# Routing weights of an expert layer: from a spreading matmul to a store and broadcast loads

## The chip, the cores and the metric

The kernel runs on one core of a Trainium2 chip. The metric is the device time of one execution in microseconds (us), as the median of several executions. Everything is float32 in memory; "F32R" tiles are float32 values rounded to what TensorE multiplies in one pass, so that a product of two such tiles split in a high and a low part takes three matmuls.

## The reference

Three layers work on 32 sequences of 128 tokens of width 128 (4096 tokens). The first is a state-space mixer, the second a cross attention with 16 heads, the third a layer of experts; each ends in a residual sum and a layer norm. The change lies in the third:

```
scores = sigmoid(xf @ gate_w.T)                  # 16 experts
# two of four groups of experts stay open, the best 4 experts of those are taken
topk_w = topk_w / (topk_w.sum(-1) + 1e-20) * 2.5
cw     = (one_hot(topk_idx) * topk_w).sum(1)     # 16 weights per token, 12 of them zero
act    = silu(xf @ Wg) * (xf @ Wu)               # 16 experts of 64 units
y      = einsum(act, cw, Wd) + shared expert     # 128 units, no weight
out    = layernorm(x + (x + y))
```

All experts are computed for all tokens; the routing weight `cw` scales the 64 units of each expert before the product with `Wd`.

## The kernel before, in words

The 32 sequences are worked in 8 groups of 4 (512 tokens); in the expert stage a tile is 128 units by 512 tokens. The units are cut into 9 chunks (`NC`) of 128: chunk 0 is the shared expert, chunks 1 to 8 hold two experts each. Five engines run their own in-order programs, tied by semaphores only.

For each chunk c, **TensorE** (`up`, from L1952) makes the gate product and the up product, three matmuls each (L1957), into two PSUM banks each (`GG`, `UU`), and for c > 0 one matmul more (L1962) that spreads the two rows of routing weights over 64 rows each into a third pair of banks (`WW`). The left operand of that one is a constant 0/1 matrix `spread`, the right one `cwT`, the transposed routing weights. Two chunks later `down` (L1965) multiplies the finished hidden chunk with the down weights (L1973). So TensorE's order is up(c), down(c-2). **ScalarE** makes silu of the gate bank (L1879). **VectorE** (`hidden`) multiplies silu with the up bank (L1912), waits for that result, and multiplies it with the spread weights (L1916).

The routing of group g+1 is made between the chunks of group g. `x2T` transposes the next tokens (L1781) after chunk 2, from a tile `xs` that SyncE loaded from the SBUF tensor `x2` (L1845); ScalarE copies and rounds the transposed tokens (L1679, L1682), VectorE makes their low part (L1699); `expert_logits` (L1788) follows chunk 3. On VectorE `expert_scores` and `rank_groups` stand behind chunk 3, `select_experts` (L1747 to L1757) behind chunk 5, `share_weights` (L1767 to L1776) behind chunk 7. Its last two instructions split `cw` in two parts. TensorE transposes both parts (`transpose_weights`, L1796) after up(g+1, 0); ScalarE copies the result to `cwT` (L1694). After the 9 chunks VectorE makes residual sum and statistics (L124, L131, L135), GpSimd normalises (L141 to L148), SyncE stores (L1851).

In the expert stage SyncE's program of group g is: load `xs` of group g+2, wait for the normalised group g, store it. The loop over groups is `pairs`: three turns of a hardware loop of two groups, and two groups unrolled.

The routing of group 0 is made in the last group of the attention stage: VectorE routes ahead of `invert`, TensorE transposes at the end of `group`, ScalarE copies after `context`. In the attention stage GpSimd also prepares for the experts: `prepare_pool` in group 4 builds `spread` in the memory of the raw weights, `load_weights` in group 5 starts the loads of the expert weights, `split_weights` splits the up and gate weights into high and low parts (L1669, L1672).

`Sem.at(g, k)` is the count that a semaphore has once step k of group g is done.

Of the kernel before, what the change touches and what calls it, by code (L numbers as in the profile page):

```python
# [44 lines left out]
SPREAD, PREPARED = 6, 12  # L45
# [940 lines left out]
def attention(nc, t, d, psum, a, e):  # L986
# [12 lines left out]
    with ExitStack() as ctx:  # L999
# [97 lines left out]
        def _(pool):  # L1097
# [80 lines left out]
        def _(act):  # L1178
            for s in (a_exp, a_mt, a_ctx, *d_m, *d_ms, e.a_x, e.a_l, e.a_c, e.a_f):
                s.prime(act)  # L1180
# [32 lines left out]
            def group(g, par, left):  # L1213
# [32 lines left out]
                if not left:  # L1246
                    copy_weights(act, e, 0, 0)
# [143 lines left out]
        def _(pe):  # L1391
            for s in (p_v, p_s, p_t, p_u, p_c, p_mt, p_o, p_b, e.p_x, e.p_l, e.p_c, e.p_u, e.p_w):
                s.prime(pe)
# [124 lines left out]
            def group(g, par, left):  # L1518
# [23 lines left out]
                weigh(g, par, 2, 1)  # L1542
                if left >= 2:
                    values(g + 2, par)
# [10 lines left out]
                if not left:  # L1555
                    transpose_weights(pe, e, 0)
# [36 lines left out]
def expert_tensors(ctx, nc, t, psum, a):  # L1593
# [9 lines left out]
    e.w_raw = sb("w_raw", [P, 2, NC, P])  # L1603
    e.w_up = sb("w_up", [P, 2, 2, NC, P], F32R)
# [4 lines left out]
    e.spread = sb("spread", [P, CHUNKS, P], F32R)  # L1609
    e.before = sb("before", [P, 4, 4])  # L1610
    e.xT_hl = [sb("xT_hl_c0", [P, 2, GT], F32R)]
    e.cwT = [sb(f"cwT{k}", [P, GT], F32R) for k in range(2)]
# [10 lines left out]
    e.cw, e.cw_hl = sb("cw", [P, GS, EXPERTS]), sb("cw_hl", [P, GS, 2, EXPERTS], F32R)  # L1623
# [3 lines left out]
    e.p_u, e.p_w = sem("up_mm", NC), sem("weight_mm", CHUNKS)  # L1627
    e.a_x, e.a_l, e.a_c, e.a_f = sem("x2T_hi"), sem("logit_tanh"), sem("cwT_ready"), sem("x2T_f32")
    e.v_x, e.v_sc, e.v_grp, e.v_sel = sem("x2T_lo"), sem("scores_ready", 2), sem("groups_ranked", 13), sem("select_dve", 18)
# [3 lines left out]
def prepare_pool(pool, e, pick):  # L1633

    before, steps = e.before, e.steps
    pool.memset(pick[:, :, :, :], 1.0).then_inc(steps, 1)
    pool.memset(before[:, :, :], 1.0).then_inc(steps, 1)
    pool.wait_ge(steps, 2)

    pool.affine_select(out=pick[:, :, :, :], in_=pick[:, :, :, :], compare_op=ALU.is_equal, fill=0.0, base=0,  # L1640
                       pattern=[[-2, CHUNKS], [-1, 2], [0, EI]], channel_multiplier=1).then_inc(steps, 1)
    pool.affine_select(out=before[:, :, :], in_=before[:, :, :], compare_op=ALU.is_gt, fill=0.0, base=0,
                       pattern=[[1, 4], [-1, 4]], channel_multiplier=0).then_inc(steps, 1)
    pool.wait_ge(steps, 4)
    pool.affine_select(out=pick[:, :, :, :], in_=pick[:, :, :, :], compare_op=ALU.not_equal, fill=1.0, base=-EXPERTS,
                       pattern=[[-2, CHUNKS], [-1, 2], [0, EI]], channel_multiplier=1).then_inc(steps, 1)
    pool.wait_ge(steps, 5)
    pool.tensor_copy(e.spread[:, :, :], pick[:, :, :, :].rearrange("p c e i -> p c (e i)")).then_inc(steps, 1)
    for cwT in e.cwT:
        pool.memset(cwT[:, :].bitcast(F32), 0.0).then_inc(steps, 1)  # L1650
# [13 lines left out]
def split_weights(pool, e):  # L1664
# [5 lines left out]
    pool.wait_ge(steps, 10)  # L1670
# [90 lines left out]
def share_weights(dve, e, g):  # L1761

    def step(k, ins):
# [8 lines left out]
    step(15, dve.scalar_tensor_tensor(e.cw[:, :, :], e.chosen[:, :, :], SCALE, bc(e.wsum[:, :, None], [P, GS, EXPERTS]),  # L1772
                                      ALU.mult, ALU.mult))
# [18 lines left out]
def transpose_weights(pe, e, g):  # L1792
    pe.wait_ge(e.v_sel.sem, e.v_sel.at(g, 17))
# [270 lines left out]
```

## Time and profile before

| what | us |
|---|---|
| median of 3 executions | 636.02 (634.12 to 638.72) |
| the profiled execution | 634.59 |
| its span, first to last instruction | 632.9 |
| TensorE busy in the span | 576.1 (91%) |
| VectorE busy | 481.5 (76%) |
| ScalarE busy | 279.6 (44%) |
| GpSimd busy | 205.7 (33%) |
| mean granted TensorE clock | 0.969 of full |

Busy shares are means over the three stages. The expert stage runs from 430.65 us, its first gate matmul, to the end. The page's row of memory traffic shows 114 to 205 GB/s in the attention stage and mostly 0 to 34 GB/s in the expert stage.

### The profile page before, as it was taken

What the parts mean: (1) busy time and instruction counts of PE and PEld (TensorE: products, weight loads), DVE (VectorE), ACT (ScalarE), POOL (GpSimd) and SP (SyncE); (2) the same over time, 40 slices, a digit from 0 to 9 for tenths busy, and PEclk for the clock granted to TensorE, in tenths of its full rate; (3) what the DMA queues carried; (4) which work ended last, traced back from release to release, by engine and by line L of the source; (5) the groups of instructions that cost most, each with busy time, mean ns of one, the idle gap of its engine ahead of it and who ended that gap; (6) DMA issues with size and microseconds to landing.
All of it is one profiled execution on the core that took longest, in us unless ns stands there. A gap on an engine that the chain in (4) does not pass through costs nothing. (4 is left out here: it accounts for less than half of the span.)

```text
span 632.9 us, 17897 instructions
## 1 busy us (share of the span) xinstructions
PE 576.1 (91%) x6280; PEld 480.9 (76%) x6280; DVE 481.5 (76%) x1174; ACT 279.6 (44%) x548; POOL 205.7 (33%) x256
## 2 busy tenths in 40 slices
PE   5769999999999866999999999788999999999994
PEld 5647876887888655787878877567888888888884
DVE  2858888888988758687787788665787787887863
ACT  2356645645655423565575555343233223233220
POOL 4233224314412574325434547732022022021022
PEclk9969999999999967999999999799999999999998
DMA  7122122022111473544545545000010010110000
GB/s 225 58 66 86 48 67 66 33 66 66 53 58 40 114 205 89 142 136 143 156 144 151 140 124 171 5 4 34 2 34 6 28 33 0 33 33 0 18 18 17
DMA packets 43086, 46.13 MB, mean 73 GB/s; under 512 B 5056, under 2 KB 31328, under 8 KB 43024
## 3 DMA queue, kind: packets, MB, share of 16 engines
q1 hardware_dynamic: 41104, 42.57, 22.5%
q0 software_dynamic: 704, 1.92, 1.0%
q10 hardware_dynamic: 1216, 0.79, 0.5%
q8 instruction: 41, 0.67, 0.4%
q14 instruction: 21, 0.17, 0.1%
HBM read 32.48 MB, written 10.94 MB: 69 GB/s over the span
## 5 line engine op out<-in xcount | busy, mean ns | idle before, releaser
L1957 PE MATMUL bank<-xT_hl_c,w_up 128*128 128x512 f32 x432 | 118.1, 409 | 2.4 <-ACTq L67 2.4
L141 POOL TENSOR_TENSOR rstd<-mv,norm_c 128x4 f32<-128x4 f32 x24 | 5.2, 216 | 289.2 <-DVE mv L135 188.4
L1879 ACT ACTIVATE sg<-bank 128x512 f32<-128x512 f32 x72 | 42.9, 596 | 105.0 <-PE bank L1957 105.0
L1957 PEld LDWEIGHTS bank<-xT_hl_c,w_up 128*128 128x128 f32 x432 | 76.1, 189 | 15.8 <-ACTq L67 2.6
L1282 DVE TENSOR_REDUCE nmax<-bank 128x4 f32<-128x512 f32 x112 | 72.0, 685 | 20.6 <-PE bank L1439 19.3
L1186 ACT ACTIVATE prob<-bank 128x512 f32<-128x512 f32 x128 | 69.4, 595 | 40.8 <-PE bank L1439 33.0
L1973 PEld LDWEIGHTS bank<-w_down,hid 128*128 128x128 f32 x576 | 74.4, 191 | 5.9 <-issue 0.5
L1973 PE MATMUL bank<-w_down,hid 128*128 128x128 f32 x576 | 75.6, 275 | 0.0
L1912 DVE TENSOR_TENSOR gu<-sg,bank 128x512 f32<-128x512 f32 x64 | 43.9, 685 | 21.4 <-PE bank L1957 10.2
L1429 PE MATMUL bank<-neg_i,mask 64*128 64x256 bf16 x512 | 51.2, 279 | 9.1 <-DVE nmax L1290 3.0
L1916 DVE TENSOR_TENSOR hid<-gu,bank 128x512 f32<-128x512 f32 x64 | 44.0, 688 | 6.5
L477 ACT ACTIVATE expo<-rows,neg_sums 128x128 f32<-128x128 f32 x128 | 40.8, 390 | 11.2 <-DVE mix L855 11.1
L422 PE MATMUL bank<-xhl,w_feat 128*128 128x512 f32 (+1 forms) x96 | 31.4, 452 | 9.0 <-DVE b_rot L814 5.1
L1479 PE MATMUL bank<-prob,ones_s 128*32 128x128 f32 x1024 | 34.6, 276 | 0.5 <-ACT prob L1186 0.5
L1429 PEld LDWEIGHTS bank<-neg_i,mask 64*128 64x128 bf16 x512 | 16.4, 95 | 23.8 <-issue 9.8
L1483 PE MATMUL bank<-prob,v_d 128*32 128x128 f32 x1024 | 34.4, 275 | 0.0
L919 PE MATMUL bank<-c_rot,b_rot 128*128 128x256 f32 x128 | 32.9, 378 | 0.0
L1479 PEld LDWEIGHTS bank<-prob,ones_s 128*32 128x32 f32 x1024 | 26.0, 109 | 5.7 <-issue 2.2
L916 PE MATMUL bank<-plain 96*128 96x512 f32 x96 | 30.0, 420 | 0.0
L908 PEld LDWEIGHTS bank<-w_x,xhl 128*128 128x128 f32 x192 | 26.8, 189 | 3.8 <-issue 1.2
L422 PEld LDWEIGHTS bank<-xhl,w_feat 128*128 128x128 f32 (+1 forms) x96 | 16.9, 186 | 16.7 <-DVE c_rot L818 7.6
L908 PE MATMUL bank<-w_x,xhl 128*128 128x256 f32 x192 | 28.6, 285 | 0.0
(220 smaller groups left out, 1184.7 us busy)
## 6 DMA issues: line engine op xcount, KB each, us to landing
rows<-sum_rows_scratch SPq DMA_DIRECT2D x32, 256.0 KB, 3.2
k_stack<-k_scratch SPq DMA_DIRECT2D x32, 128.0 KB, 2.8
q_stack<-q_scratch SPq DMA_DIRECT2D x32, 128.0 KB, 2.7
k_scratch<-k_part SPq DMA_DIRECT2D x16, 192.0 KB, 2.4
q_scratch<-q_part SPq DMA_DIRECT2D x16, 192.0 KB, 2.4
x<-xT_in SPq DMA_DIRECT2D x8, 256.0 KB, 8.6
mask<-mask_in SPq DMA_DIRECT2D x8, 256.0 KB, 3.0
xres<-x_in SPq DMA_DIRECT2D x8, 256.0 KB, 3.7
```

The source lines that it names most:

```text
L422: mm = pe.matmul(bank[0:m, :], w[:, i, :], xhl[:, par, v, :, 1:], start=(n == 0), stop=(n == 2))
L477: act.activation(expo[:, b % 2, h, :], rows[:, b, h, :], ACT.Exp, bias=upto_s[:, bass.ds(g * GS + b, 1), h]).then_inc(s_exp.sem, 1)
L908: mm = pe.matmul(bank[:, shift * D_INNER:(shift + 1) * D_INNER], xhl[:, par, a, b, 1 - shift:P + 1 - shift], w_x[:, v, :], start=(n == 0), ...
L1186: act.activation(prob[:, b % 2, ORDER[n], :, :], (TT0, TT1)[n % 2][:, :], ACT.Exp, scale=XD ** -0.5)\
L1282: dve.tensor_reduce(nmax[:, b, 4 * u:4 * u + 4], (SS0, SS1)[n % 2][:, :].rearrange("p (i k) -> p i k", i=4), AX_X, ALU.max, negate=True).t ...
L1429: pe.matmul(banks[j][:, :].rearrange("p (i h k) -> p i h k", i=4, h=2)[:, :, half, :], mask[rows, par, b, kind + ver, :], bc(neg_i[rows, N ...
L1479: mm = pe.matmul(U1[32 * u:32 * u + 32, 0:P], ones_s[:, 4 * b + i, :, :].rearrange("p r c -> p (r c)"), prob[:, b % 2, u, i, :], start=(b ...
L1879: act.activation(sg[:, k, :], GG[k][:, :], ACT.Silu).then_inc(a_s.sem, 1)
L1912: dve.tensor_tensor(dst, sg[:, k, :], UU[k][:, :], ALU.mult).then_inc(v_gu.sem, 1)
L1916: dve.tensor_tensor(hid[:, c, :], gu[:, k, :], WW[(c - 1) % 2][:, :], ALU.mult).then_inc(v_hid.sem, 1)
L1957: mm = pe.matmul(bank[:, :], w_up[:, which, a, c, :], xT_hl[par][:, v, :], start=(n == 0), stop=(n == 2))
L1973: mm = pe.matmul(PO[:, b * P:(b + 1) * P], hid[:, c, b * P:(b + 1) * P], w_down[:, c, :], start=(c == 0 and b == 0), stop=(c == NC - 1), s ...
```

## The change

- `spread`, its building on GpSimd, the spreading matmuls and the split of `cw` in two parts are gone; `cw` is transposed as it is, to 16 rows.
- ScalarE copies the 16 x 512 transposed weights to SBUF and stores them to DRAM from its own queue. SyncE loads them back as `share`: each row to 64 partitions, in eight loads of 256 KB per group (for each of four pairs of chunks one load to partitions 0 to 63, one to 64 to 127). The loads stand ahead of the load of `xs` in SyncE's program, and each pair of loads waits until VectorE has used the pair's old content.
- VectorE multiplies by `share` instead of by a PSUM bank.
- Gate and up products have three banks each.
- `select_experts` stands behind chunk 4 (before 5), `share_weights` behind chunk 5 (before 7), `transpose_weights` and the copy behind chunk 7 (before: after up(g+1, 0)). In the last attention group the transposes stand ahead of the last two products `weigh(g, par, 3, ...)`, the copy ahead of `context`.
- VectorE's loop over the groups is unrolled.

```
@@ attention, gpsimd / scalar / tensor, last groups @@
                 if left == 2:
-                    pool.wait_ge(e.steps, SPREAD)
                     load_weights(pool, d, e)
...
-                        prepare_pool(pool, e, e.w_raw[:, 0, 0:CHUNKS, :].rearrange("p c (x y) -> p c x y", x=2))
+                        prepare_pool(pool, e)
...
+                if not left:
+                    copy_weights(act, e, 0, 0)
                 context(g)
...
                 weigh(g, par, 2, 1)
+                if not left:
+                    transpose_weights(pe, e, 0)
                 if left >= 2:
                     values(g + 2, par)
                 weigh(g, par, 3, 1)
...
 def prepare_pool(pool, e):
-    (memset, two affine_select and a copy of 128x1024 for spread, two memsets of cwT)
     pool.memset(before[:, :, :], 1.0).then_inc(steps, 1)
...
 def copy_weights(act, e, g, par):
     act.wait_ge(e.p_c.sem, e.p_c.at(g))
-    act.wait_ge(e.p_w.sem, e.p_w.at(g - 2, CHUNKS - 1))
-    act.activation(e.cwT[par][0:32, :], e.PF[0:32, :], ACT.Copy).then_inc(e.a_c.sem, 1)
+    act.wait_ge(e.d_stored.sem, e.d_stored.at(g - 1))
+    act.activation(e.cw_rows[:, :], e.PF[0:EXPERTS, :], ACT.Copy).then_inc(e.a_c.sem, 1)
+    act.wait_ge(e.a_c.sem, e.a_c.at(g))
+    act.dma_start(e.cw_dram[par], e.cw_rows[:, :]).then_inc(e.d_stored.sem, 16)
...
 def share_weights(dve, e, g):
-    step(16, dve.tensor_copy(e.cw_hl[:, :, 0, :], e.cw[:, :, :]))
-    step(17, dve.tensor_tensor(e.cw_hl[:, :, 1, :], e.cw[:, :, :], e.cw_hl[:, :, 0, :].bitcast(F32), ALU.subtract))
...
-        GG, UU, WW, PF, PO = psum[0:2], psum[2:4], psum[4:6], psum[6], psum[7]
+        GG, UU, PF, PO = psum[0:3], psum[3:6], psum[6], psum[7]
@@ experts, sync @@
+            def load_shares(g, par):
+                sp.wait_ge(e.d_stored.sem, e.d_stored.at(g))
+                by_half = e.cw_dram[par].rearrange("(c j) t -> j c t", j=2)
+                for q, loaded in enumerate(d_share):
+                    sp.wait_ge(v_hid.sem, v_hid.at(g - 1, 2 * q + 1))
+                    for j in range(2):
+                        sp.dma_start(share[EI * j:EI * j + EI, 2 * q:2 * q + 2, :],
+                                     by_half[j, 2 * q:2 * q + 2].partition_broadcast(EI)).then_inc(loaded.sem, 16)
             def group(g, par, left):
+                if left:
+                    load_shares(g + 1, 1 - par)
                 if left == 2:
                     load(g + 2, par)
                 sp.wait_ge(g_out.sem, g_out.at(g, 3))
...
+            load_shares(0, 0)
             load(1, 1)
@@ experts, vector @@
-                    dve.wait_ge(p_w.sem, p_w.at(g, c - 1))
-                    dve.tensor_tensor(hid[:, c, :], gu[:, k, :], WW[(c - 1) % 2][:, :], ALU.mult)
+                    dve.wait_ge(d_share[(c - 1) // 2].sem, d_share[(c - 1) // 2].at(g))
+                    dve.tensor_tensor(hid[:, c, :], gu[:, k, :], share[:, c - 1, :], ALU.mult)
...
-            pairs(dve, group)
+            for g in range(NG):
+                group(g, g % 2, min(2, NG - 1 - g))
@@ experts, tensor @@
-                    pe.wait_ge(freed.sem, freed.at(g, c - 2))
+                    pe.wait_ge(freed.sem, freed.at(g, c - 3))
...
-                    pe.matmul(WW[(c - 1) % 2][:, :], spread[:, c - 1, :], cwT[par][:, :], start=True, stop=True)
...
+                    if left and c == 7:
+                        transpose_weights(pe, e, g + 1)
                 if left:
                     up(*nxt, 0)
-                    transpose_weights(pe, e, g + 1)
                 down(g, NC - 2)
```

## Rows read from the trace of the kernel before

**Rows 1.** Busy time per stretch: busy us (instructions) of PE, PEld, DVE, ACT, POOL; clock, DMA share, GB/s.
```profile
456.00:481.00 25.00, 25.00 (x155) 21.83 (x154) 20.62 (x66) 7.32 (x13) 3.25 (x4) 1.00 0.07 23
```

**Rows 2.** Chain that ended last, 552 to 602 us: start us, us, what.
```profile
552.29 0.61 PE bank L1796 x4
...
597.10 1.40 PE bank L1957 x6
598.49 0.23 PE bank L1962
...
601.02 0.44 PE bank L1796 x4
```

**Rows 3.** Timeline of VectorE in the second group: start us, us, engine, line, [idle before].
```profile
459.16 0.68 DVE L124 SCALAR_TENSOR_TENSOR res<-x,bank 128x512 f32<-128x512 f32 x1
...
462.96 0.69 DVE L1699 TENSOR_TENSOR xT_hl_c<-rest,xT_hl_c 128x512 fp32r<-128x512 f32 x1 [0.19 <-ACT xT_hl_c L1682]
...
469.00 0.69 DVE L1912 TENSOR_TENSOR gu<-sg,bank 128x512 f32<-128x512 f32 x1 [0.29 <-PE bank L1957]
...
471.82 0.22 DVE L1747 TENSOR_TENSOR open_<-biased,penalty 128x64 f32<-128x64 f32 x1
...
473.93 0.69 DVE L1912 TENSOR_TENSOR gu<-sg,bank 128x512 f32<-128x512 f32 x1 [0.30 <-ACT sg L1879]
...
476.76 0.19 DVE L1767 TENSOR_SCALAR chosen<-marked 128x64 f32<-128x64 f32 x1
...
477.91 0.22 DVE L1772 SCALAR_TENSOR_TENSOR cw<-chosen,wsum 128x64 f32<-128x64 f32 x1
...
478.40 0.23 DVE L1776 TENSOR_TENSOR cw_hl<-cw,cw_hl 128x64 fp32r<-128x64 f32 x1
```

**Rows 4.** Timeline of TensorE and of ScalarE in the second group, same columns.
```profile
460.96 0.60 PE L1781 MATMUL bank<-ident,xs_c 128*128 128x128 f32 x4
...
479.58 0.59 ACT L1694 ACTIVATE cwT<-bank 32x512 fp32r<-32x512 f32 x1 [0.54 <-PE bank L1796]
```

**Rows 5.** Timeline of SyncE's queue: issues in the first stage, and at the expert stage's start.
```profile
25.73 0.56 SPq L456 DMA_DIRECT2D sum_rows_scratch<-sum_rows  x1
27.60 1.76 SPq L461 DMA_DIRECT2D rows<-sum_rows_scratch  x4
...
430.62 4.05 SPq L1845 DMA_DIRECT2D xs_c<-x  x2
```

**Rows 6.** The broadcast loads of the first stage (one tile's view), and a stretch of them.
```profile
DMA to landing us min/median/max: 3.0/3.2/5.6
...
30.00:31.00 1.00, 1.00 (x5) 0.69 (x4) 0.51 (x2) 0.98 (x2) 0.32 (x1) 1.00 0.98 363
```

**Rows 7.** A stretch of loads that land on 32 or on 16 partitions each.
```profile
238.00:240.00 2.00, 0.78 (x18) 0.42 (x12) 2.00 (x4) 0.63 (x1) 1.19 (x1) 1.00 1.03 211
```

**Rows 8.** Issues by line: KB each, median us to landing.
```profile
xs_c<-x SPq DMA_DIRECT2D x7, 256.0 KB, 2.3
```

**Rows 9.** Timeline of GpSimd, VectorE and TensorE in attention groups 4 and 5.
```profile
375.98 0.95 POOL L1636 MEMSET w_raw<- 128x1024 f32 x1
...
381.73 0.20 POOL L141 TENSOR_TENSOR rstd<-mv,norm_c 128x4 f32<-128x4 f32 x1
...
398.38 5.23 POOL L1672 TENSOR_TENSOR w_up<-w_raw,w_up 128x1152 fp32r<-128x1152 f32 x2
...
401.12 2.54 DVE L1306 TENSOR_TENSOR npart<-nrest,npart 128x32 bf16<-128x32 f32 x1
...
403.81 0.38 PE L1503 MATMUL bank<-ident,npart 128*48 128x128 bf16 x2 [3.85 <-DVE npart L1306]
```

**Rows 10.** A stretch right after that wait of TensorE, columns as in Rows 1.
```profile
404.00:409.00 5.00, 5.00 (x38) 4.02 (x37) 1.21 (x2) 2.31 (x5) 4.25 (x4) 0.50 0.02 5
```

**Rows 11.** Timeline of TensorE and VectorE in the last attention group.
```profile
422.48 1.08 PE L1479 MATMUL bank<-prob,ones_s 128*32 128x128 f32 x32 [0.16 <-ACT prob L1186]
...
423.00 0.23 DVE L1772 SCALAR_TENSOR_TENSOR cw<-chosen,wsum 128x64 f32<-128x64 f32 x1
```

More of the change, by code:

```diff
@@ L44 @@
 SENTINEL, TAKEN = -3.0e38, 3.0e38
-SPREAD, PREPARED = 6, 12
+PREPARED = 6
 TWO_ONES = 1 + 0x3F80 / 2**23
@@ L1178, in _ @@
         def _(act):
-            for s in (a_exp, a_mt, a_ctx, *d_m, *d_ms, e.a_x, e.a_l, e.a_c, e.a_f):
+            for s in (a_exp, a_mt, a_ctx, *d_m, *d_ms, e.a_x, e.a_l, e.a_c, e.a_f, e.d_stored):
                 s.prime(act)
@@ L1391, in _ @@
         def _(pe):
-            for s in (p_v, p_s, p_t, p_u, p_c, p_mt, p_o, p_b, e.p_x, e.p_l, e.p_c, e.p_u, e.p_w):
+            for s in (p_v, p_s, p_t, p_u, p_c, p_mt, p_o, p_b, e.p_x, e.p_l, e.p_c, e.p_u):
                 s.prime(pe)
@@ L1554, in group @@
                 output(g)
-                if not left:
-                    transpose_weights(pe, e, 0)
             def first_scores(b, p):
@@ L1603, in expert_tensors @@
     e.w_raw = sb("w_raw", [P, 2, NC, P])
+    e.cw_rows = sb("cw_rows", [EXPERTS, GT])
+    e.cw_dram = nc.dram_tensor("cw_scratch", (2, EXPERTS, GT), F32, kind="Internal").ap()
     e.w_up = sb("w_up", [P, 2, 2, NC, P], F32R)
@@ L1608, in expert_tensors @@
     e.bias = sb("bias", [P, EXPERTS])
-    e.spread = sb("spread", [P, CHUNKS, P], F32R)
     e.before = sb("before", [P, 4, 4])
     e.xT_hl = [sb("xT_hl_c0", [P, 2, GT], F32R)]
-    e.cwT = [sb(f"cwT{k}", [P, GT], F32R) for k in range(2)]
     e.th16 = sb("th16", [P, GS, EXPERTS])
@@ L1669, in split_weights @@
         pool.tensor_copy(w_up[:, k, 0], w_raw[:, k]).then_inc(steps, 1)
-    pool.wait_ge(steps, 10)
+    pool.wait_ge(steps, 4)
     for k in range(2):
@@ L1815, in raw @@
             return ctx.enter_context(nc.semaphore(name))
-        w_up, w_down, spread, xT_hl, cwT = e.w_up, e.w_down, e.spread, e.xT_hl, e.cwT
+        w_up, w_down, xT_hl = e.w_up, e.w_down, e.xT_hl
         xT_hl.append(sb("xT_hl_c1", [P, 2, GT], F32R))
@@ L1822, in experts @@
         hid = sb("hid", [P, NC, GT])
+        share = sb("share", [P, CHUNKS, GT])
         res, stats, mv, rstd = t["res"], t["stats"], t["mv"], t["rstd"]
@@ L1827, in experts @@
         d_x, d_out = DmaSem(ctx, nc, "x2_staged"), DmaSem(ctx, nc, "out_stored")
-        p_x, p_u, p_w, a_c = e.p_x, e.p_u, e.p_w, e.a_c
+        d_share = [sem(f"share_loaded{q}", 1, 32) for q in range(CHUNKS // 2)]
+        p_x, p_u, a_c = e.p_x, e.p_u, e.a_c
         p_g, p_d, a_s = sem("gate_mm", NC), sem("down_mm", NC), sem("silu_ready", NC)
@@ L1841, in _ @@
             d_out.prime(sp)
+            for loaded in d_share:
+                loaded.prime(sp)
+            def load_shares(g, par):
[6 more added lines that the diff above has]
+                                     by_half[j, 2 * q:2 * q + 2].partition_broadcast(EI)).then_inc(loaded.sem, 16)
             def load(g, par):
@@ L1926, in group @@
                         rank_groups(dve, e, g + 1)
+                    if left and c == 4:
+                        select_experts(dve, e, g + 1)
                     if left and c == 5:
-                        select_experts(dve, e, g + 1)
-                    if left and c == 7:
                         share_weights(dve, e, g + 1)
@@ L1952, in up @@
             def up(g, par, c):
-                k = (par + c) % 2
-                for which, bank, freed, done in ((0, GG[k], a_s, p_g), (1, UU[k], v_gu, p_u)):
-                    pe.wait_ge(freed.sem, freed.at(g, c - 2))
+                for which, bank, freed, done in ((0, GG[c % 3], a_s, p_g), (1, UU[c % 3], v_gu, p_u)):
+                    pe.wait_ge(freed.sem, freed.at(g, c - 3))
                     for n, (a, v) in enumerate(((0, 0), (0, 1), (1, 0))):
@@ L1958, in up @@
                     mm.then_inc(done.sem, 1)
-                if c:
-                    pe.wait_ge(a_c.sem, a_c.at(g))
-                    pe.wait_ge(v_hid.sem, v_hid.at(g, c - 3))
-                    pe.matmul(WW[(c - 1) % 2][:, :], spread[:, c - 1, :], cwT[par][:, :], start=True, stop=True)\
-                        .then_inc(p_w.sem, 1)
             def down(g, c):
@@ L1985, in group @@
                         expert_logits(pe, e, g + 1)
+                    if left and c == 7:
+                        transpose_weights(pe, e, g + 1)
                 if left:
                     up(*nxt, 0)
-                    transpose_weights(pe, e, g + 1)
                 down(g, NC - 2)
```

39 lines of the change are left out of this document (13 added, 26 removed).

## The prediction

> **What bounds the kernel now.** I read the busy time per stretch first, then the chain of waits, then each engine's timeline in one group of the expert stage. TensorE is busy for 25.00 of 25.00 us in a stretch of that stage, VectorE for 20.62 [rows 1], so only what leaves TensorE's path or lands on it counts. The chain is TensorE alone: the transposes of the routing weights recur at 552.29 and, two groups later, at 601.02 [rows 2], a period of 24.37 us. A chunk on it is the gate and up products 1.40, the spreading matmul 0.23, and down; between 597.10 and 601.02 stand up, spread, down, up, so down is 3.92 - 1.40 - 0.23 - 1.40 = 0.89 [rows 2].
>
> **What is removed.** Eight spreading matmuls per group, 8 x 0.23 = 1.87 us, would leave a period of 22.5 if TensorE stayed the bound. VectorE loses two small instructions, 478.13 to 478.63 [rows 3], 0.5 us. Its multiplication doesn't get quicker: with one operand in PSUM it takes 0.69, with both in SBUF also 0.69 (L1699) [rows 3].
>
> **What is added, as a cycle.** I follow one group from the end of cw on VectorE (call it S, before at 477.91 + 0.22 = 478.13) to the S of the next group, because three new waits stand in that cycle one behind the other.
>
> 1. Transposes and ScalarE's copy: from the last routing instruction, 478.40 + 0.23, to the copy's end, 479.58 + 0.59, are 1.54 us [rows 3, 4].
> 2. Store and the issue of the first load: the first stage has the same pair, store issued at 25.73, first broadcast load at 27.60, 1.87 us [rows 5]. The load is issued at S + 3.4.
> 3. Eight loads of 256 KB, then, in the same queue, the 256 KB of xs that TensorE transposes for the next group but one. A broadcast load there lands 3.2 us after its issue in the median, and the stretch with several in flight moves 363 GB/s [rows 6], so 0.72 us of the 3.2 are data and 2.48 are fixed. With d us of data per load, xs lands at S + 3.4 + 2.48 + 9d = S + 5.9 + 9d. SyncE issues four loads in 1.76 us [rows 5], 0.44 each, so d decides as long as it is larger. The last pair also waits for VectorE's last chunk of the running group, three chunks behind S, some 4.2 us (3 x 1.41, below), which is over when its turn comes.
> 4. Transpose, two copies on ScalarE, start of L1699: 460.96 to 462.96, 2.00 us [rows 4, 3].
> 5. From there VectorE has one serial program to the next S. L1699, chunk 3 and the ranking: 462.96 to 469.00, 6.04. Chunk 4: half of 469.00 to 471.82, 1.41. Selection: 471.82 to 473.93, 2.11. Chunk 5: half of 473.93 to 476.76, 1.42. The shares: 476.76 to 478.13, 1.37. Sum 12.35 [rows 3].
>
> The new period is 5.9 + 9d + 2.00 + 12.35 = **20.24 + 9d**, if xs is what TensorE waits for. It is: behind the transposes TensorE has four ups and four downs before it needs xs, 0.44 + 4 x 1.40 + 4 x 0.89 = 9.6 us after S. Even at the highest rate of the trace, d = 0.72, xs lands at S + 12.4. Before, this load stood at the head of the group's program; now its issue comes some 7 us after S, and its data queue behind 2 MB.
>
> **The value of d.** No row has loads of 64 rows. Those of 128 rows moved 363 GB/s at a DMA share of 0.98 [rows 6]; those of 32 and of 16 rows (line 276) moved 211 GB/s at 1.03 [rows 7], the engines as full and the bytes fewer: 1.24 us per 256 KB. Between 0.72 and 1.24 I take 1.1, nearer to the narrow loads, because a load that reaches only half of the rows resembles them more, and the wider of them is half as wide. Period: 20.24 + 9.9 = 30.1, against 24.37.
>
> The Trainium skill has a rule on this, "SBUF — State Buffer", section "Door 1: The DMA port swizzle": 64 partitions reach 8 of the 16 ports, as 32 do, and two loads on the two halves run almost one after the other. Its table has 196 GB/s for 64 rows, d = 1.34, by which the same sum, clock term included, would give about 694 us.
>
> **The sum.** In group 0 the shares are loaded as the stage starts, ahead of xs of group 1. By the issue at 430.62 [rows 5], xs lands at 430.62 + 2.48 + 9.9 = 443.0, the first S is 2.00 + 12.35 later, 457.35, and the seventh six periods later, 457.35 + 6 x 30.14 = 638.2. What follows has no routing and TensorE sets it. Before, 31.9 us lay from the last transposes to the end (632.9 - 601.02); now the transposes stand one up, one down and one more up sooner (3.7) and eight spreading matmuls go (1.87): 33.7. The span ends at 671.9, +39.0.
>
> **The attention stage.** GpSimd's building of the spreading matrix stood ahead of its normalisation, 375.98 to 381.73 [rows 9]; nearly all of it goes, so that the weights load and split sooner. The second half of the split ran from 398.38 for 5.23 us while VectorE's small L1306 took 2.54, and TensorE waited 3.85 us for it [rows 9]. An earlier split holds VectorE for a shorter time; bounds 0 and 3.85, I take -2.5 (half of the 5.75 is swallowed by GpSimd's other waits). Against it, the transposes of group 0 now stand ahead of the last products, which began at 422.48, and wait for cw, finished at 423.23 [rows 11]; with 0.44 of their own they delay what follows by about 1.2. Net -1.3, bounds -3.85 and +1.2.
>
> **The clock.** TensorE would wait 15.8 - 9.6 = 6.2 us for xs in each group. After its wait of 3.85 us [rows 9] the granted clock of the next stretch is 0.50, the 1.2 GHz level [rows 10]. The work from xs to the scores then takes longer: an up and a down, 2.29, would cost 2.29 more. Bounds 0 and 2.3 per group; I take 1 in 7 groups, since VectorE's own work covers part: +7.
>
> **Costed at nothing.** The copy and the issue on ScalarE ahead of silu(8): ScalarE works 7.32 of 25 us [rows 1]; 0.6 per group if silu were late. VectorE's unrolled loop: it is hidden by the wait for xs; without that, not more than 0.3 per group, the gaps of its timeline [rows 3]. Three banks: TensorE can't run further ahead, since down(c-2) still waits for VectorE; no gain. The small weight store and the output store, behind xs in the queue, have a group's time.
>
> Profiled execution 634.59 + 39.0 - 1.3 + 7 = **679 us**; that execution lies 1.4 below the median shown, too little to correct for.
>
> **The rivals.**
> - *Full-rate loads* (0.15): the same late xs, but 64 rows run as 128 do, d = 0.72. Period 26.7, S at 453.9 and 614.3, end 648.0, and a wait of 2.8 us without a clock loss: 634.6 + 15.0 - 1.3 = 648. For it: 363 GB/s was reached with the same kind of source. Against it: rows 7.
> - *The halves never overlap* (0.13): a load to one half of the rows holds all engines until it is done, and 64 rows run at the 211 GB/s of the narrow loads, d = 1.24 [rows 7]. Period 31.4, S at 458.6 and 647.0, end 680.7; with the clock term 688. For it: the engines' full share in those rows. Against it: they contain loads of 16 rows. It is the rule of the Trainium skill's "SBUF — State Buffer", "Door 1: The DMA port swizzle", above.
> - *xs overtakes* (0.07): issued at S + 3.4 + 8 x 0.44 = S + 6.9 and landing 2.3 later [rows 8], it is there at 9.2, just in time. Then VectorE waits for the first pair of shares, S + 3.4 + 2.48 + 2d = 8.1, multiplies (0.6), makes residual and chunk 2 (459.16 to 462.96, 3.8) and the 12.35: period 24.9, no better than before, since routing behind chunks 3, 4 and 5 leaves TensorE little to do in the first half of a group. 634.6 + 6 x 0.5 - 1.9 - 1.3 = 634.
> - *Faster: TensorE stays the bound* (0.09): period 22.5, 8 x 1.87 = 15 us less, 634.6 - 15 - 1.3 = 618. It decides if xs is there by S + 9.6, that is d below 0.42 (620 GB/s in one queue), or if it overtakes and VectorE's serial part is 2.4 shorter than its rows make it. For it: VectorE has 4.4 us of idle time per 25 [rows 1], which three banks might let it use.
>
> **How the numbers follow.** The forecast has 0.56. Its own range, d from 0.9 to 1.2 with a clock term from 0 to 14, is 660 to 692. The range of 8 in 10 takes in both rivals on loads, from 644 (full rate and the whole gain of attention) to 695. Faster by over 1% 0.09, within 1% 0.07, slower 0.84; 1% is about what runs of this kernel, 634.12 to 638.72, tell from no change.
>
> **What would show it.** In the changed kernel: xs issued behind eight share loads and landing well over 2.3 us later; TensorE's transposes (L1781 before) waiting some 6 us per group for it, and VectorE's low part behind them; a period near 30; share loads at 210 to 260 GB/s with the DMA share near 1; a granted clock under 1 in the expert stage. A period under 25 with TensorE busy throughout would prove me wrong, and xs on time would prove the mechanism wrong.

## The result, and the profile after

The changed kernel takes 678.8 us in the median of 4 runs (675.77 to 679.85), against 635.53 for the kernel before on the same chip. The ratio is 1.0666, 95% interval 1.0632 to 1.0701: slower by 43 us. The forecast was 679. The profiled execution is one of 679.48 us with a span of 677.7.

Four views carry the reading. First busy time per stretch, columns as in [rows 1]: one whole period of the expert stage, the stretch in which its loads land, and the one after TensorE's wait.

```profile
456.07:487.41 31.34, 25.51 (x143) 21.68 (x143) 19.59 (x63) 7.38 (x13) 3.56 (x4) 0.89 0.37 86
...
462.70:471.30 8.60, 3.38 (x22) 2.60 (x20) 4.75 (x13) 0.60 (x1) 3.56 (x4) 0.91 0.98 213
...
472.00:477.00 5.00, 5.00 (x22) 4.42 (x20) 2.07 (x3) 1.78 (x3) 0.00 (x0) 0.55 0.18 52
```

TensorE, without a gap in [rows 1], now has work for 25.51 us of 31.34. While the loads land the DMA engines are full (0.98) and move 213 GB/s, close to the 211 GB/s of the narrow loads in [rows 7] and far from the 363 GB/s of [rows 6]. Behind the wait the granted clock is 0.55, near the lower of the two levels (1.2 GHz); in [rows 1] it was 1.00.

Second the waits: engine, line, what it waited for, us in total, times, longest. Third the issues by line, as in [rows 8], and the share of each line in the chain that ended last.

```profile
DVE xT_hl_c L1689 <- ACT xT_hl_c L1670: 39.7, 7, 7.0
PE bank L1769 <- DMA xs_c<-x: 34.5, 7, 5.3
...
DVE hid L1920 <- DMA share<-cw_scratch: 6.5, 7, 1.5
```

```profile
share<-cw_scratch SPq DMA_DIRECT2D x64, 256.0 KB, 5.6
...
xs_c<-x SPq DMA_DIRECT2D x7, 256.0 KB, 7.0
...
cw_scratch<-cw_rows ACTq DMA_DIRECT2D x8, 32.0 KB, 1.6
```

```profile
DMA xs_c<-x 7%; SPq L1840 5%; PE bank L1961 5%; PE bank L1972 3%; DVE gu L1916 2%; DVE hid L1920 2%; DMA cw_scratch<-cw_rows 1%; PE bank L1769 1%; PE bank L1776 1%; DVE marked L1747 1%; DMA share<-cw_scratch 1%; PE bank L1784 1%; ACT cw_rows L1682 1%; DVE top L1742 0%; DVE chosen L1758 0%
```

The waits that cost are not those for the new loads (6.5 us in seven groups) but those for xs, which queues behind them: 34.5 us on TensorE, 39.7 on VectorE one step later. The load that landed 2.3 us after its issue [rows 8] now takes 7.0, and it has the largest share of the chain.

Fourth the timelines of one cycle, VectorE, TensorE, ScalarE and SyncE, in the order of the forecast's steps; they answer to [rows 3 to 5].

```profile
455.79 0.22 DVE L1763 SCALAR_TENSOR_TENSOR cw<-chosen,wsum 128x64 f32<-128x64 f32 x1
...
456.07 0.60 PE L1784 MATMUL bank<-ident,cw 128*16 128x128 f32 x4
...
456.80 0.59 ACT L1682 ACTIVATE cw_rows<-bank 16x512 f32<-16x512 f32 x1 [2.11 <-PE bank L1784]
...
457.41 0.31 ACTq L1684 DMA_DIRECT2D cw_scratch<-cw_rows  x1
...
459.07 5.27 SPq L1840 DMA_DIRECT2D share<-cw_scratch  x8
...
464.61 0.54 SPq L1845 DMA_DIRECT2D xs_c<-x  x1
...
465.93 1.13 PE L1972 MATMUL bank<-w_down,hid 128*128 128x128 f32 x8 [0.98 <-DVE res L124]
...
471.68 1.11 PE L1769 MATMUL bank<-ident,xs_c 128*128 128x128 f32 x4 [4.62 <-DMA xs_c<-x]
472.44 2.91 PE L1961 MATMUL bank<-xT_hl_c,w_up 128*128 128x512 f32 x6
...
474.18 0.69 DVE L1689 TENSOR_TENSOR xT_hl_c<-rest,xT_hl_c 128x512 fp32r<-128x512 f32 x1 [5.15 <-ACT xT_hl_c L1670]
487.41 0.60 PE L1784 MATMUL bank<-ident,cw 128*16 128x128 f32 x4
```

S is 455.79 + 0.22 = 456.01. xs is issued 8.6 us later and TensorE can start on it at 471.68, S + 15.7. From transposes to transposes it is 31.34 us; from the first cw of the stage at 455.79 to the seventh at 641.60 the mean period is 30.97.

The attention stage, same view of GpSimd, VectorE and TensorE, answers to [rows 9, 11].

```profile
375.16 0.11 POOL L1635 MEMSET before<- 128x16 f32 x1
...
393.94 5.22 POOL L1660 TENSOR_TENSOR w_up<-w_raw,w_up 128x1152 fp32r<-128x1152 f32 x2
...
399.67 0.19 DVE L1305 TENSOR_TENSOR npart<-nrest,npart 128x32 bf16<-128x32 f32 x1
...
400.62 0.29 PE L1502 MATMUL bank<-ident,npart 128*48 128x128 bf16 x2
...
418.46 0.60 PE L1784 MATMUL bank<-ident,cw 128*16 128x128 f32 x4 [0.96 <-DVE cw L1763]
...
427.04 6.76 PE L1961 MATMUL bank<-xT_hl_c,w_up 128*128 128x512 f32 x18 [2.79 <-ACTq L67]
```

L1305, which took 2.54 us in [rows 9], takes 0.19, and TensorE's 3.85 us of waiting are gone. A wait of 0.96 us for `cw`, by the sooner transposes, is new.

### The profile page after: what moved, and what is told of

Its sections match the earlier page's. It is cut to its first block and busy times, and to the rows that moved or that the text cites. A ratio compares the mean times of both kernels' runs of the same rounds, so it can differ in the third digit from the quotient of the medians.

```text
span 677.7 us, 17557 instructions
## 1 busy us (share of the span) xinstructions
PE 579.4 (85%) x6216; PEld 478.5 (71%) x6216; DVE 477.2 (70%) x1158; ACT 279.6 (41%) x548; POOL 202.6 (30%) x250
## 5 line engine op out<-in xcount | busy, mean ns | idle before, releaser
L1961 PE MATMUL bank<-xT_hl_c,w_up 128*128 128x512 f32 x432 | 128.9, 438 | 2.8 <-ACTq L67 2.8
L1961 PEld LDWEIGHTS bank<-xT_hl_c,w_up 128*128 128x128 f32 x432 | 83.5, 207 | 18.3 <-ACTq L67 2.9
L1972 PEld LDWEIGHTS bank<-w_down,hid 128*128 128x128 f32 x576 | 77.2, 198 | 18.1 <-issue 6.3
L1185 ACT ACTIVATE prob<-bank 128x512 f32<-128x512 f32 x128 | 69.4, 594 | 41.5 <-PE bank L1438 32.4
L1972 PE MATMUL bank<-w_down,hid 128*128 128x128 f32 x576 | 79.1, 282 | 6.5 <-DVE res L124 5.8
L1920 DVE TENSOR_TENSOR hid<-gu,share 128x512 f32<-128x512 f32 x64 | 47.4, 741 | 8.4 <-DMA share<-cw_scratch 6.5
L477 ACT ACTIVATE expo<-rows,neg_sums 128x128 f32<-128x128 f32 x128 | 40.8, 390 | 11.1 <-DVE mix L855 11.0
L1769 PE MATMUL bank<-ident,xs_c 128*128 128x128 f32 x28 | 7.8, 433 | 34.5 <-DMA xs_c<-x 34.5
L1689 DVE TENSOR_TENSOR xT_hl_c<-rest,xT_hl_c 128x512 fp32r<-128x512 f32 x8 | 5.5, 688 | 39.7 <-ACT xT_hl_c L1670 39.7
L1769 PEld LDWEIGHTS bank<-ident,xs_c 128*128 128x128 f32 x28 | 5.0, 217 | 35.8 <-DMA xs_c<-x 20.4
```

The costliest lines, as they stand in the source:

```text
L477: act.activation(expo[:, b % 2, h, :], rows[:, b, h, :], ACT.Exp, bias=upto_s[:, bass.ds(g * GS + b, 1), h]).then_inc(s_exp.sem, 1)
L1185: act.activation(prob[:, b % 2, ORDER[n], :, :], (TT0, TT1)[n % 2][:, :], ACT.Exp, scale=XD ** -0.5)\
L1920: dve.tensor_tensor(hid[:, c, :], gu[:, k, :], share[:, c - 1, :], ALU.mult).then_inc(v_hid.sem, 1)
L1961: mm = pe.matmul(bank[:, :], w_up[:, which, a, c, :], xT_hl[par][:, v, :], start=(n == 0), stop=(n == 2))
L1972: mm = pe.matmul(PO[:, b * P:(b + 1) * P], hid[:, c, b * P:(b + 1) * P], w_down[:, c, :], start=(c == 0 and b == 0), stop=(c == NC - 1), s ...
```

## The experiments

Ratios are to the kernel before, run on the same chip.

**The order of the queue.** The load of xs is issued ahead of the eight share loads, in the loop and at the start.

```
-                if left:
-                    load_shares(g + 1, 1 - par)
                 if left == 2:
                     load(g + 2, par)
+                if left:
+                    load_shares(g + 1, 1 - par)
...
+            load(1, 1)
             load_shares(0, 0)
-            load(1, 1)
```

> The changed kernel with one edit: SyncE issues the load of xs ahead of the eight share loads, in the loop and at the stage's start. Theory (xs is late because it queues behind 2 MB of share loads): TensorE's wait for xs, 4.6 to 5.1 us a group, goes, the granted clock of the expert stage comes back to 1.0, and the next limit is the first pair of shares and VectorE's serial part, a period of 24 to 25 us against 31.3; total 626 to 634, below the changed kernel by some 48. Rival A (the order of the routing, behind chunks 3, 4 and 5, costs the time, and the wait for xs only hides it): the period falls to 28 at best, total 650 or more. Rival B (the share loads' own traffic slows everything): hardly any change, 670 to 679.

It took 633.67 us, ratio 0.9975 (0.9950 to 1.0000), not clearly different from the kernel before. One place in a program is the whole loss of 43 us. TensorE has no wait for xs left, its load lands 2.4 us after the issue, and the mean period is 24.63. The place decides two things at once, which this run doesn't separate: what xs queues behind, and when it is issued, which is no longer after the wait for the store. The share loads were as slow as in the changed kernel: a landing every 1.17 us in both. VectorE's waits for them are what is left, and in one period the clock is back at 1.00:

```profile
xs_c<-x SPq DMA_DIRECT2D x7, 256.0 KB, 2.4
...
DVE hid L1920 <- DMA share<-cw_scratch: 6.4, 8, 1.5
...
474.10:499.30 25.20, 23.20 (x142) 19.67 (x142) 20.13 (x63) 7.32 (x13) 3.57 (x4) 1.00 0.43 106
```

**Width of a load, first try.** Each load fills one chunk, two rows of weights to all 128 partitions, the source given as 2 x 64 x 512; alone, and with xs first.

```
-                    for j in range(2):
-                        sp.dma_start(share[EI * j:EI * j + EI, 2 * q:2 * q + 2, :],
-                                     by_half[j, 2 * q:2 * q + 2].partition_broadcast(EI)).then_inc(loaded.sem, 16)
+                    for c in (2 * q, 2 * q + 1):
+                        two = e.cw_dram[par, 2 * c:2 * c + 2, :]
+                        sp.dma_start(share[:, c, :], two[:, None, :].to_broadcast([2, EI, GT])).then_inc(loaded.sem, 16)
```

> The changed kernel with one edit: the same eight loads of 256 KB and the same contents, but each load brings one chunk to all 128 partitions instead of two chunks to 64. Theory (d, the data time of a load, is set by how many partitions it reaches): a load takes 0.72 to 0.8 us instead of the 1.16 between two landings of the changed kernel, xs lands 3.2 to 4 us sooner, the period is 20.24 + 9 x 0.75 = 27 us, total 640 to 652. Rival (reading the same 2 KB of DRAM 64 times sets the rate, or the issue on SyncE of 0.65 us): loads stay at 1.1 us or more, total 672 to 680.

> Both edits: xs first and share loads to 128 partitions. Theory: with xs out of the way the rate of the share loads matters only for VectorE's wait for the first pair of shares, about 1 us a group: 1 to 3 us less than xs first alone, 624 to 631. Rival (the loads' rate matters for itself): 8 us or more below xs first alone.

They took 936.55 us, ratio 1.4722 (1.4654 to 1.4790), and 795.71, ratio 1.2527 (1.2465 to 1.2589). Every range was missed, by some 165 us at the least. The busy time per stretch, and the tile's view of the issues (engine, count, duration in ns min/median/max), of the first of the two:

```profile
427.00:500.00 73.00, 31.39 (x160) 26.11 (x159) 18.87 (x55) 9.86 (x17) 2.69 (x3) 0.71 0.10 38
```

```profile
L1840 SPq DMA_DIRECT2D share<-cw_scratch x64: 498/4979/7296, 426.9 to 901.9; - x64
```

The engines are 0.10 busy on the mean of 16 and move 38 GB/s while everything waits, and one issue takes up to 7.3 us. The Trainium skill, "DMA: Bandwidth & Descriptors", "Why a DMA increments its semaphore by 16 and not by 1", says that a transfer is split over the largest number of engines, up to 16, that divides the slowest dimension of source and destination both. By that the source's slowest dimension of 2 leaves 2 engines of 16, 0.125, and 0.10 agrees; which engines were busy no row here shows. By the rate alone these two runs changed another thing than the width, and they say nothing of it.

**Width of a load, second try.** One row of weights goes to all 128 partitions, so that both sides have 128 as their slowest dimension. The second expert of each pair is left out, so the output is not that of the reference.

```
+                    for c in (2 * q, 2 * q + 1):
+                        sp.dma_start(share[:, c, :], e.cw_dram[par, 2 * c, :].partition_broadcast(P)).then_inc(loaded.sem, 16)
```

> The changed kernel, with its 256 KB loads one row to all 128 partitions instead of two rows to 64 (the weights of each pair's second expert are left out and the first's used in their place). Theory (the half-width destination is what makes a load take 1.16 us on the queue): spacing falls to about 0.72 us, as in the full-width load that moved 363 GB/s [rows 6]; the staging load lands 8 x 0.44 = 3.5 us sooner, its wait on TensorE falls from 4.6 to about 1.1 us, period 31.3 - 3.5 = 27.8, time 679 - 7 x 3.5 = 654 (648 to 660). Rival A (256 KB written take 1.16 us whatever the width): 679 (675 to 683). Rival B (a broadcast source keeps it off most of the engines, as in the run with two rows in one load): above 750.

It took 662.94 us, ratio 1.0438 (1.0390 to 1.0487), between the theory and rival A. The stretch from the first landing to the last:

```profile
459.70:466.30 6.60, 3.76 (x24) 2.98 (x22) 4.75 (x13) 1.00 (x2) 2.52 (x3) 0.96 0.98 280
```

With the engines as full as before (0.98) they move 280 GB/s instead of 213; over all groups a load lands every 0.89 us instead of 1.17. The mean period is 28.52, 2.45 shorter: 7 x 0.28 = 1.96 for the spacing, the rest for a first landing 3.0 to 3.4 us after its issue instead of 3.6 to 4.0. So the width costs, as the theory had it, though a load now also reads one row of weights instead of two, which no run separates. The gain was seven tenths of the 3.5 forecast. The 363 GB/s [rows 6] are the mean of 1 us; the three loads that land around it come 0.77 and 0.80 us apart, so 0.72 was too low a price even there.

**Another queue for xs.** ScalarE issues the load behind the second silu of the next group.

```
                     silu(*nxt, 1)
+                if left == 2:
+                    act.wait_ge(p_x.sem, p_x.at(g))
+                    act.dma_start(xs[:, par, :, :], x2[:, bass.ds((g + 2) * GS, GS), :]).then_inc(d_x.sem[par], 16)
```

> The changed kernel, with the staging load issued by ScalarE behind the second silu of the next group, at nearly the same time (S + 8.9) but in another queue. Theory (the load waits for its turn behind the eight share loads in SyncE's queue): in a queue of its own it shares the engines and lands about S + 12 to 13 instead of S + 15.6, TensorE's wait falls by about 3 us of 4.6, time 679 - 7 x 3 = 658 (650 to 665). Rival A (it is the engines that are busy, in the order in which the requests came, whatever queue they came from): 679 (675 to 683). Rival B (ScalarE's issue holds up the silus): above 685.

It took 665.76 us, ratio 1.0463 (1.0417 to 1.0510), 0.8 above the theory's range. In the group that answers to the one above (S = 456.72):

```profile
459.78 5.34 SPq L1840 DMA_DIRECT2D share<-cw_scratch  x8
...
462.92 0.60 ACTq L1897 DMA_DIRECT2D xs_c<-x  x1
...
469.75 1.11 PE L1769 MATMUL bank<-ident,xs_c 128*128 128x128 f32 x4 [2.51 <-DMA xs_c<-x]
```

TensorE's wait for xs falls from 4.62 to 2.51 us. Two things changed, not one: ScalarE issued xs at S + 6.2, where the expectation had S + 8.9 and the changed kernel S + 8.6, and from issue to landing it still takes 6.8 us, against 7.0. So the run doesn't tell the queue from the sooner issue in the 13 us gained. What the other queue does is seen in the order: xs lands 2.8 us ahead of the last share load (2.2 to 3.4 over the groups) instead of 0.3 behind it, and the share loads spread to one per 1.30 us. It shares the same busy engines (0.93 of them from 463.5 to 472.4 us). The Trainium skill, "DMA: Bandwidth & Descriptors", "Queues, rings and completion order", has each engine take packets from its queues in turn; this run agrees.

**Routing where it was.** Selection, shares, transposes and copy go back to their old places; loads and multiplication stay.

```
-                    if left and c == 4:
+                    if left and c == 5:
                         select_experts(dve, e, g + 1)
-                    if left and c == 5:
+                    if left and c == 7:
                         share_weights(dve, e, g + 1)
```

(and so for the transposes and the copy, behind the next group's first up and first silu).

> The changed kernel with the routing put back to its old places: selection behind chunk 5, shares behind chunk 7, transposes after the gate and up products of the next group's chunk 0, copy after its silu. Everything else stays. Theory (the cycle through store, share loads and xs is the bound): weights that are ready two chunks later start the loads later, VectorE then waits some 4 to 5 us for the first pair of shares, period 33 to 35, total 692 to 710. Rival (routing sooner is what costs): period falls, total below 670.

It took 703.1 us (two runs), ratio 1.1056 (1.0987 to 1.1124), as expected. The sooner routing is worth 24 us here:

```profile
PE bank L1769 <- DMA xs_c<-x: 32.2, 7, 5.9
DVE hid L1919 <- DMA share<-cw_scratch: 30.6, 7, 4.6
```

The wait for xs stays what it was, and VectorE waits for the first shares on top of it. The two waits stand in the same cycle one behind the other.

**The clock.** TensorE makes 18 spare matmuls into the free bank while it waits for xs.

```
+                pe.wait_ge(a_c.sem, a_c.at(g - 1))
+                for _ in range(18):
+                    pe.matmul(e.PF[:, :], w_up[:, 0, 0, 0, :], xT_hl[1 - par][:, 0, :], start=True, stop=True)
                 pe.wait_ge(d_x.sem[par], d_x.at(g, par))
-                pe.wait_ge(a_c.sem, a_c.at(g - 1))
```

> The changed kernel, with 18 spare matmuls of 128x512 on TensorE while it waits for the staging load. Theory (about 1.3 us of each period is the half clock after that wait: transposes 1.11 for 0.60, up 2.91 for 1.64): the granted clock stays at full speed, period 31.3 - 1.3 = 30.0, time 679 - 7 x 1.3 = 670 (667 to 674). Rival A (what is late lies on the transfers and VectorE, not on TensorE's speed): 679 (676 to 682). Rival B (18 x 0.22 = 4 us of matmuls outlast the wait of 4.6 us after some groups): 680 to 690.

It took 667.42 us, ratio 1.0517 (1.0468 to 1.0565). The last row is busy time per stretch, from the spare matmuls to the end of the period.

```profile
466.65 4.45 PE L1955 MATMUL bank<-xT_hl_c,w_up 128*128 128x512 f32 x18
471.63 0.66 PE L1769 MATMUL bank<-ident,xs_c 128*128 128x128 f32 x4 [0.53 <-DMA xs_c<-x]
472.05 1.66 PE L1963 MATMUL bank<-xT_hl_c,w_up 128*128 128x512 f32 x6
...
466.60:487.00 20.40, 19.66 (x114) 16.26 (x113) 13.94 (x51) 4.97 (x10) 3.57 (x4) 1.00 0.23 54
```

xs is no sooner than in the changed kernel, but the granted clock behind it is 1.00 and the up takes 1.66 us instead of 2.91. Spare work made the kernel 11 us faster by the medians; the mean period is 29.13, so the half clock had cost 1.84 per group. What lies between xs and the scores is TensorE's own work, at whatever clock it gets.

**The attention stage.** The removed preparation on GpSimd is put back, for nobody's use, with the waits that it had.

```
-PREPARED = 6
+SPREAD, PREPARED = 6, 12
...
+    pool.memset(pick[:, :, :, :], 1.0).then_inc(steps, 1)
...
+    pool.tensor_copy(e.spread[:, :, :], pick[:, :, :, :].rearrange("p c e i -> p c (e i)")).then_inc(steps, 1)
+    for cwT in e.cwT:
+        pool.memset(cwT[:, :].bitcast(F32), 0.0).then_inc(steps, 1)
```

> The changed kernel, with GpSimd's removed preparation put back (the spread matrix is built and two tensors are cleared, for nobody; loading and splitting the expert weights wait for it as before). Theory (this work is what delayed the split weights, VectorE and TensorE in the attention's last groups): stage start goes back from 427.0 to 430.6, time 679 + 3.6 = 682.5 (681.5 to 684). Rival (the sooner routing and the other order of the last group made the 3.6 us): 679 (678 to 680).

It took 682.83 us, ratio 1.0751 (1.0712 to 1.0790), above the changed kernel's interval; by the medians that is 4.0 us. The old wait is back:

```profile
375.59 0.95 POOL L1638 MEMSET w_raw<- 128x1024 f32 x1
...
403.63 0.38 PE L1503 MATMUL bank<-ident,npart 128*48 128x128 bf16 x2 [3.31 <-DVE npart L1306]
...
431.82 4.43 PE L1975 MATMUL bank<-xT_hl_c,w_up 128*128 128x512 f32 x18 [2.79 <-ACTq L67]
```

From the start of GpSimd's preparation to the start of the expert stage the three kernels have 54.67 (before), 51.88 (after) and 56.23 us (this one). By these three traces the removed work is worth 4.35, and the new order of the last group costs 56.23 - 54.67 = 1.56. The 1.56 is loose: in the eleven other kernels with the attention stage of the changed one the stretch is 51.5 to 52.8 us in ten and 54.45 in one.

**No loads at all.** In the changed order the share loads are made for the first group alone; the others multiply by its weights.

```
+                    if first:
                         for j in range(2):
...
+                    else:
+                        sp.sem_inc(loaded.sem, 32)
```

> The changed kernel in the order that it has, but the share loads are made for the first group alone (the later groups multiply by the first group's weights); their places in SyncE's queue, the waits for the store and for the buffers stay. Theory (everything that the change lost, it lost to these transfers): the staging load lands 2.4 us after its issue, no wait for it on TensorE, period about 24.5, time 631 (625 to 635), 1 to 3 us below the run with the staging load first. Rival (the cycle of transposes, store and VectorE is long by itself): above 645.

It took 636.42 us, ratio 1.0002 (0.9972 to 1.0031): 1.4 above the range, and 2.8 above the run with xs first instead of 1 to 3 below it. Group 0 still has its loads ahead of xs, and TensorE its wait of 4.9 us behind them: from the first `cw` to the second it is 36.26 us, against 28.71 with xs first. In the loop behind it the theory held, and the period says more. The first two rows are busy time per stretch, one period of this run and one of the kernel before. The others are products of `hidden` beside GpSimd's normalisation, two from the run with xs first and then one from the kernel before:

```profile
481.22:505.00 23.78, 23.08 (x143) 19.69 (x144) 20.22 (x63) 7.31 (x13) 3.57 (x4) 1.00 0.08 24
...
478.13:502.79 24.66, 24.66 (x153) 21.69 (x152) 19.61 (x65) 7.41 (x14) 3.31 (x4) 1.00 0.07 21
```

```profile
485.95 1.04 POOL L142 TENSOR_TENSOR res<-res,mv 128x512 f32<-128x512 f32 x1
...
486.35 1.19 DVE L1920 TENSOR_TENSOR hid<-gu,share 128x512 f32<-128x512 f32 x1
...
488.48 1.04 POOL L148 TENSOR_TENSOR normed<-res,rstd 128x512 f32<-128x512 f32 x1
...
488.79 1.28 DVE L1920 TENSOR_TENSOR hid<-gu,share 128x512 f32<-128x512 f32 x1
```

```profile
487.93 1.11 POOL L148 TENSOR_TENSOR normed<-res,rstd 128x512 f32<-128x512 f32 x1
...
488.85 0.69 DVE L1916 TENSOR_TENSOR hid<-gu,bank 128x512 f32<-128x512 f32 x1
```

With transfers that cost nothing the period is 23.78, against a mean of 24.21 before. TensorE works 23.08 of it. So nothing like 8 x 1.87 us was to be had in this order of the work: about 0.4 per group. VectorE is a likely part of the reason. It lost two instructions, yet it is busy for 20.22 us of this period and was for 19.61 of one before. Two of its eight products of `gu` and `share`, both in SBUF, take 1.19 and 1.28 us beside GpSimd instead of 0.69, and about as long in the run without loads: 1.1 us per group. With the second operand in PSUM such a product took 0.69 in the kernel before. In the run without loads TensorE also waits for VectorE's product in front of the transposes (3.5 us in six groups), and VectorE then for a silu (1.6 us a group). No run takes the two slow products away by themselves, so what they cost the kernel isn't shown.

**A version that beats both?** Three were tried on top of xs first: the shares of chunks 3 to 8 multiplied by GpSimd; the staging of x2 and the routing one chunk sooner; and with it TensorE's down products three chunks behind the up products.

```
+                for c in range(3, NC):
+                    pool.wait_ge(v_gu.sem, v_gu.at(g, c))
+                    pool.wait_ge(d_share[(c - 1) // 2].sem, d_share[(c - 1) // 2].at(g))
+                    pool.tensor_tensor(hid[:, c, :], gu[:, (par + c) % 2, :], share[:, c - 1, :], ALU.mult).then_inc(g_hid.sem, 1)
```

> The staging load ahead of the share loads, as in the run of 633.67, and the multiplications by the share of chunks 3 to 8 moved from VectorE to GpSimd, which has 4.4 us of work in a period of 24.9. Theory (there VectorE sets the period: 18 multiplications of 0.69, 4 further ones, about 6 us of routing and 2.1 of residual; a GpSimd product of this size takes 1.04 to 1.30 us): VectorE loses 6 x 0.71 = 4.2 us, TensorE becomes the bound at 9 x 2.29 + 2.2 = 22.8, time 633.7 - 7 x 2.1 = 619 (612 to 626). Rival A (the two engines get in each other's way in SBUF, as where a VectorE product takes 1.19 to 1.28 instead of 0.69): 628 to 640. Rival B (the longer chain from silu over two engines to the down product makes TensorE wait): above 640.

```
                     if left and c == 2:
-                        x2T(*nxt)
-                    if left and c == 3:
                         expert_logits(pe, e, g + 1)
...
                 down(g, NC - 1)
+                if left == 2:
+                    x2T(g + 2, par)
```

> The staging load first, as in the run of 633.67, and with it in hand early the transposes of x2, their copies and split, the logits and the ranking are moved one chunk sooner (x2 behind chunk 1 of the group before, logits and ranking behind chunk 2). Theory (with the load out of the way VectorE and TensorE share the bound; in that run VectorE idles 1.6 + 1.5 us of each period just ahead of the routing and is full behind it, where TensorE waits 0.5 to 0.8 us for products): routing moves into the idle stretch, period 24.9 - 0.7 to 2, time 633.7 - 5 to 14 = 626 (620 to 630). Rival (the idle stretch is the wait for the first share loads, which the store starts: it moves along with the routing): 633 (630 to 637).

```
-                for c in range(2, NC):
+                for c in range(3, NC):
                     up(g, par, c)
-                    down(g, c - 2)
...
-                    if left and c == 7:
+                    down(g, c - 3)
+                    if left and c == 8:
                         transpose_weights(pe, e, g + 1)
```

> The kernel with the staging one chunk sooner, and besides TensorE's down products three chunks behind the up products instead of two, the transposes of the weights behind chunk 8. Theory (the rest of the period is TensorE waiting for VectorE's products right in front of the transposes): TensorE's waits go, period towards 9 x 2.29 + 0.36 + 0.8 + 0.36 = 22.1, time 1 to 8 us below the kernel that it is built on (618 to 628). Rival (VectorE, not TensorE's order, sets the period): equal to it within 2 us, or slower by the transposes that come 2.3 us later.

With products on GpSimd it took 636.68 us, ratio 1.0005 (0.9973 to 1.0037), in the range of rival A. VectorE was relieved of six products and the mean period stayed at 24.60:

```profile
471.38 1.32 DVE L1758 TENSOR_TENSOR chosen<-chosen,score 128x64 f32<-128x64 f32 x1
...
471.32 1.30 POOL L1878 TENSOR_TENSOR hid<-gu,share 128x512 f32<-128x512 f32 x1 [1.11 <-DVE gu L1927]
```

A product of 64 columns that takes 0.23 us elsewhere lasts until the GpSimd product that began just before it is over, and this one stands in the routing, on the cycle. Rival B's mechanism is there too, at a lower price than it had: TensorE waits 5.3 us in six groups, up to 1.0 at a time, for a product of GpSimd. The Trainium skill, "SBUF — State Buffer", "Who interferes with whom", says that a VectorE instruction with two inputs in SBUF contends with a GpSimd instruction that reads SBUF; the two rows agree.

One chunk sooner, it took 633.29 us, ratio 0.9938 (0.9914 to 0.9963), clearly under the kernel before, by 0.6%. That lies in the rival's range and 3.3 above the theory's, and the mean period fell only from 24.63 to 24.42; against xs first alone (0.9950 to 1.0000) the intervals overlap, so a gain over that kernel isn't shown. Three chunks behind, it took 633.72, ratio 0.9955 (0.9935 to 0.9975), also under the kernel before and equal to one chunk sooner, as its rival had it:

```profile
DVE hid L1921 <- DMA share<-cw_scratch: 21.7, 8, 3.8
```

VectorE now waits 21.7 us in all for shares, against 5.2 without the third chunk of lag. The first pair lands some 8 us after S in both, and VectorE's product starts 0.1 us behind it: VectorE comes to the shares sooner and waits longer.

## Why the prediction was right, point by point

**The likeliest case came out**, with its mechanism: queue order, full engines, a late xs and three waits in one cycle. The run with xs first shows that the place of xs costs the 43 us, and the run without loads that the loop loses nothing but by the transfers. That the number was hit to 0.2 us is luck: the last S came 2.1 us sooner than forecast and the end 2.2 us later behind it.

- *Steps 1 and 2.* S to the first load's issue: 3.06 us, forecast 3.4.
- *Step 3.* First issue to the landing of xs: TensorE starts 471.68 - 459.07 = 12.61 later; forecast 2.48 + 9.9 = 12.4. Two errors cancel in it: d is 1.17 instead of 1.1, but xs lands 0.3 to 0.6 us after the last share load, not a whole d later. SyncE needs 0.66 per issue (5.27 / 8) where I took 0.44; d is larger, so it didn't matter. The Trainium skill, "SBUF — State Buffer", "Can I just issue two DMAs to hit both halves?", has two loads on two halves run one behind the other; the rate of 213 GB/s with alternating halves agrees. The forecast names "Door 1: The DMA port swizzle" for this too, but the sentence on two loads stands in the section named here. The price by that page's table in the forecast, d = 1.34, was too dear.
- *Step 4.* xs to L1689: 2.50 us, forecast 2.00, at half the clock.
- *Step 5.* VectorE's serial part: 474.18 to the next S, 487.13 + 0.23 = 487.36, 13.18 us; forecast 12.35. It now waits for TensorE's slow ups, which the clock term was to cover.
- *The clock.* Steps 4 and 5 together are 1.33 over their rows, and filling the wait won 1.84 per group; forecast 1, bounds 0 and 2.3. TensorE's wait was 4.62, not 6.2, since it reaches xs at S + 11.1 instead of S + 9.6, of which 0.98 is a wait for the residual that I had not counted.
- *The start and the end.* First S 456.0, forecast 457.35 - 1.3 + 1 = 457.05; last S 641.8, forecast 638.2 - 1.3 + 7 = 643.9. The end lies 35.9 behind it, forecast 33.7. In the run without loads it is 34.5, but also 34.8 in the run with the preparation put back, whose expert stage is that of the changed kernel. So how much of the missing 2.2 comes with the loads is open.
- *The attention stage* was mis-sized, with the right signs: -4.35 for the preparation and +1.56 for the transposes, net -2.8, where I had -2.5 and +1.2, net -1.3. I let half of GpSimd's 5.75 be swallowed by other waits; about a quarter was. The bound of 3.85 was no bound. The half clock behind that wait [rows 10] goes with it: from 405 to 415 us the granted clock is 0.78 in the kernel before and with the preparation put back, and 1.00 in the changed kernel.

**The rivals.** Full-rate loads (648) fell by the 213 GB/s, and even loads of full width take 0.89 us here and not 0.72. Of "the halves never overlap" (688) no run settles the mechanism: a load takes 1.17 us over all groups, midway between its 1.24 and the forecast's 1.1. Its time fell, since xs adds 0.3 to 0.6 us behind the last load and not a whole 1.24; with the clock term its period would be 32.4, the forecast's is 31.1, and 30.97 was measured. The late xs was real, so "xs overtakes" fell as a description of this kernel; its price, 634, is what the kernel with xs first then took. "TensorE stays the bound" (618) was not open in this order of the work: without any load the period is 23.78 and not 22.5. VectorE's serial part, which that rival needed 2.4 us shorter, is 11.82 there (493.09 to 504.91), 0.5 shorter, and the two slow products cost VectorE 1.1 us that the forecast, with 0.69 for each, had put at nothing.

## What to carry to other kernels

A transfer is priced by what stands ahead of it in its queue: ask of every added load who is issued behind it and whether that one is on the cycle, and put the small urgent load first. Price the rate by bounds from rows on either side in the spread over partitions, not by the best rate in the trace, which even loads of full width didn't reach here. Where a wait sits on TensorE, add the half-speed work behind it (here 1.84 us per group). Where an operand moves from PSUM to SBUF, look at what GpSimd does at that time.

## What the runs showed of the hardware beyond that

- Spare matmuls in a wait made the kernel faster: 667.42 against 678.8 us.
- Two broadcast loads of the same 256 KB, one row to 128 partitions or two rows to 64 each in one load, differ by the engines they use: a landing every 0.89 us at 0.98 of the engines, or 38 GB/s at 0.10.
- VectorE's new products with both inputs in SBUF take 0.69 us alone, but 1.19 and 1.28 (with xs first, at 486.35 and 488.79) beside GpSimd's normalisation.
